# A graph network on one core: edges placed into 300 of 500 columns, counts in one product, and a factor of the attribute product in PSUM

## The chip, the core and the metric

The kernel runs on 1 core of a Trainium2 chip. The core has a matmul engine (TensorE; PE in the profile), three engines for elementwise work (VectorE or DVE, ScalarE or ACT, GpSimd or POOL) and a queue of its own for transfers (SyncE, SP). They run beside each other and wait for each other by semaphores. All work in SBUF, a memory of 128 partitions; matmuls write to PSUM, eight banks of 512 floats a partition. The metric is the device time of one call in microseconds (us).

## The reference

A graph has 3125 nodes with 128 features and 53125 directed edges, sorted by destination. Each edge has one of 8 types and 16 attributes. Four graph networks follow one another with layer norms between them; what matters here, shortened:

```python
h = relu(x @ proj.T + b)
for l in range(2):                                   # L0: gated graph network
    trans = einsum('nh,tdh->tnd', h, edge_W[l])
    agg = segment_sum(trans[edge_type, src], dst)    # one message per edge, by type and sender
    h = relu(gru_cell(agg, h, ...))
...                                                  # L1: three relational layers, means per type
    norm = 1 / max(counts[type, dst], 1)
    agg = segment_sum(xw[type, src] * norm, dst)
...                                                  # L2: normalised convolution over dst -> src
by_src = segment_sum(edge_attr, src) / count         # L3: two means of the attributes,
by_dst = segment_sum(edge_attr, dst) / count         #     by sender and by receiver
out = layernorm(x + mlp(concat(x, by_src, by_dst)))
```

All is float32.

## The kernel before

Edges are handled in 52 groups of 1024 (8 tiles of 128, one edge a partition). Nodes as senders lie in 25 sender blocks of 126.

**The first loop** (52 groups, 4 per pass of a hardware loop, about 105 to 865 us) does two things. It sums the messages of layer 1, and it builds the lists that the later layers use. For group g:
- GpSimd fetches 8 tiles of messages from the table in HBM by row number (L495 through `rows_of`, eight indirect DMAs, four buffers). The row numbers are put ready by ScalarE (`stage`, L964), two groups ahead.
- VectorE builds the 0/1 matrices of sender block (L1246) and of receiver (`onehot`, L1228), and the running number of each edge in its sender block (L1249, L1259 to L1271). From the number follows the edge's slot: a lane (`slot_lane`) and a column (`slot_col`) of a 128x500 map; a sender block has 20 columns of 128 lanes. It builds the 0/1 matrix of the lane times the edge's payload (`lane1h`, L1276).
- ScalarE builds the 0/1 matrix of the column, 8 tiles of 500 columns, as relu(1 - |column number - slot_col|): eight activations (L980) and one over 4000 columns (L984).
- TensorE multiplies, in this order: running numbers (L594, L595), message sums (`msg` x `onehot`, L600), counts by type and attribute sums by receiver (`mark` x `onehot`, L605, 24 rows), counts by sender block (`sb1h` x `onehot`, L608, 25 rows), and then `place` for the group before: `lane1h` x column matrix, 8 products of 500 columns that add into bank 7 of PSUM (L580). Each float32 product shows as two matmul records, so `place` shows as 16.
- VectorE adds the message sums and the two count results to `acc` and `nodes` (L1282, L1286, L1288).

Each step waits for its inputs by semaphores (`sb_known`, `rank_mm`, `slot_known`, `tile_ready`, `lane_ready`, `placed`, `summed`, `count_mm`), and buffers come in twos or fours.

**After it** `slots` reads the map, and four layers follow (about 900 to 2700 us). Each has a first part with 125 chunks of 4 columns (x1 records built on TensorE, copied by ScalarE, stored by SP), and a second part in which GpSimd fetches records and TensorE sums them by window (L731).

**The convolution stage** (about 2770 to 3490 us) has 100 steps `g`. GpSimd fetches 5 tiles of rows for a step (L495, `gmsg`, four buffers, 500 indirect DMAs in all), VectorE builds 5 matrices (`ghot`, L1667), TensorE multiplies them (L892). Spread over the first 88 steps lie the 52 attribute groups `attr(a)`: VectorE builds the sender block matrix `hi` (L1640) and sixteen products `aprod` = hi x attributes (L1646, two buffers), ScalarE the lane matrix `alane` (L1094, L1099), and TensorE multiplies (L899, 16 records of 400 columns a group). The order is written out in the code of each engine; no scheduler changes it. A flag set by `judge` sends the kernel to a general path, which is far slower, if an edge found no place.

## Time and profile before

| | |
|---|---|
| Time, median of 3 runs | 3567.47 us (3558.71 to 3567.86) |
| Time of the profiled execution | 3572.71 us |
| its span | 3570.9 us |
| TensorE matmul busy, share of the span | 2926.1 us, 82% |
| VectorE | 2001.8 us, 56% |
| ScalarE | 1064.1 us, 30% |
| GpSimd | 1558.0 us, 44% |

The profiled execution took 1.8 us more than its span, and 5.2 us more than the median. Busy shares are means over stages of quite different kind, so they do not say what bounds a stage. In a chain of waits the words "another core or an unknown queue", and in a list of waits "remote", stand where the profile knows no releaser.

### The profile page before, as it was taken

What the parts mean: (1) busy time and instruction counts of PE and PEld (TensorE: products, weight loads), DVE (VectorE), ACT (ScalarE), POOL (GpSimd) and SP (SyncE); (2) the same over time, 40 slices, a digit from 0 to 9 for tenths busy, and PEclk for the clock granted to TensorE, in tenths of its full rate; (3) what the DMA queues carried; (4) which work ended last, traced back from release to release, by engine and by line L of the source; (5) the groups of instructions that cost most, each with busy time, mean ns of one, the idle gap of its engine ahead of it and who ended that gap; (6) DMA issues with size and microseconds to landing.
All of it is one profiled execution on the core that took longest, in us unless ns stands there. A gap on an engine that the chain in (4) does not pass through costs nothing.

```text
span 3570.9 us, 49106 instructions
## 1 busy us (share of the span) xinstructions
PE 2926.1 (82%) x16338; PEld 2340.9 (66%) x16338; DVE 2001.8 (56%) x6739; ACT 1064.1 (30%) x1751; POOL 1558.0 (44%) x1641
## 2 busy tenths in 40 slices
PE   6799999899766998878997799878997767777748
PEld 2556665555665995777996799877996544444435
DVE  5445555555446775746764777435773754545514
ACT  2465566565332112340014300242001322323201
POOL 1455545551022661005640166103662677777760
PEclk8899999999887999999999999999996888887867
DMA  6111111110475661577767777677771122222211
GB/s 236 41 42 45 43 40 45 42 43 20 143 240 174 177 174 46 190 251 219 234 174 261 233 233 233 185 245 228 230 223 38 49 51 54 51 54 51 48 46 24
DMA packets 229115, 460.27 MB, mean 129 GB/s; under 512 B 40682, under 2 KB 95338, under 8 KB 228397
## 3 DMA queue, kind: packets, MB, share of 16 engines
q0 software_dynamic: 76992, 217.59, 22.5%
q1 hardware_dynamic: 151924, 240.14, 21.0%
q8 instruction: 112, 1.84, 0.2%
q14 instruction: 87, 0.70, 0.1%
HBM read 309.93 MB, written 147.65 MB: 128 GB/s over the span
## 4 chain that ended last, share of the span: by engine, by line
PE 53%; DMA 14%; POOL 13%; issue 8%; DVE 5%; another core or an unknown queue 4%; ACT 3%; SPq 0%; DVEq 0%; ACTq 0%; POOLq 0%
PE ps L731 20%; POOL gmsg L495 13%; DMA chunks<-xs 13%; PE ps L580 10%; PE ps L717 5%; PE ps L600 2%; ACT xs L1000 2%; PE ps L605 2%; PE ps L608 2%; PE ps L706 2%; PE ps L750 1%; PE ps L765 1%; PE ps L756 1%; PE ps L666 1%
## 5 line engine op out<-in xcount | busy, mean ns | idle before, releaser
L495 POOL DMA_INDIRECT rec<-chunks,idx x596 | 580.7, 974 | 965.4 <-DMA chunks<-xs 652.4
L731 PE MATMUL ps<-dhot,rec 128*128 128x168 f32 x4768 | 718.3, 311 | 65.3 <-DMA rec<-chunks,idx 24.7
L731 PEld LDWEIGHTS ps<-dhot,rec 128*128 128x128 f32 x4768 | 695.7, 193 | 86.5 <-issue 54.2
L1494 DVE TENSOR_SCALAR dhot<-iota,dcode 128x168 f32<-128x168 f32 x2384 | 568.9, 306 | 191.7 <-PE ps L731 110.8
L706 PE MATMUL ps<-hrow,shot 126*128 126x128 f32 x4000 | 518.6, 291 | 176.7 <-ACT xs L1000 139.3
L495 POOL DMA_INDIRECT gmsg<-gcn_rows,gcn_idx x500 | 545.5, 1091 | 269.2 <-issue 148.1
L706 PEld LDWEIGHTS ps<-hrow,shot 126*128 126x128 f32 x4000 | 492.9, 204 | 202.1 <-ACT xs L1000 161.6
L495 POOL DMA_INDIRECT msg<-messages,idx_buf x416 | 398.2, 957 | 430.2 <-ACT idx_buf L964 303.8
L580 PE MATMUL ps<-big,lane1h 128*128 128x500 f32 x848 | 392.0, 604 | 40.2 <-issue 38.3
L1000 ACT ACTIVATE xs<-ps 128x512 f32<-128x512 f32 x500 | 289.6, 597 | 423.8 <-DMA chunks<-xs 307.3
L1479 DVE TENSOR_SCALAR shot<-srow,lane_no 126x512 f32<-126x512 uint8 x500 | 237.7, 485 | 312.6 <-PE ps L706 246.2
L899 PE MATMUL ps<-aprod,alane 128*128 128x400 f32 x832 | 337.0, 557 | 40.9 <-issue 36.1
L980 ACT ACTIVATE tmp<-iota,slot_col 128x500 f32<-128x500 f32 x416 | 256.3, 698 | 336.1 <-DVE slot_col L1271 171.6
L580 PEld LDWEIGHTS ps<-big,lane1h 128*128 128x128 f32 x848 | 159.4, 194 | 243.0 <-issue 243.0
L892 PE MATMUL ps<-ghot,gmsg 128*128 128x126 f32 x1000 | 165.9, 321 | 161.1 <-DMA gmsg<-gcn_rows,gcn_idx 116.6
L899 PEld LDWEIGHTS ps<-aprod,alane 128*128 128x128 f32 x832 | 175.3, 217 | 180.1 <-issue 89.4
L892 PEld LDWEIGHTS ps<-ghot,gmsg 128*128 128x128 f32 x1000 | 152.8, 230 | 186.3 <-issue 167.9
L1646 DVE TENSOR_TENSOR aprod<-ahi,amark 128x208 f32<-128x208 f32 x832 | 235.5, 357 | 1.8
L1009 ACT ACTIVATE acc<-ps,bias 128x252 f32<-128x252 f32 (+1 forms) x39 | 18.0, 461 | 701.0 <-PE ps L720 647.3
L1667 DVE TENSOR_SCALAR ghot<-iota,gcn_lo 128x126 f32<-128x126 f32 x500 | 109.3, 299 | 180.0 <-remote 119.3
L1099 ACT ACTIVATE alane<-tmp,w 128x1024 f32<-128x1024 f32 x52 | 59.7, 1149 | 484.1 <-remote 215.9
L984 ACT ACTIVATE big<-tmp,w 128x4000 f32<-128x4000 f32 x52 | 188.8, 3630 | 1.7
(239 smaller groups left out, 2861.2 us busy)
## 6 DMA issues: line engine op xcount, KB each, us to landing
chunks<-xs SPq DMA_DIRECT2D x375, 256.0 KB, 4.6
tmp<-inverse_counts SPq DMA_DIRECT2D x36, 1008.0 KB
chunks<-xs SPq DMA_DIRECT2D x125, 258.0 KB, 4.5
srow<-lanes_of_slots SPq DMA_DIRECT2D x100, 320.0 KB, 4.3
messages<-big SPq DMA_DIRECT2D x25, 504.0 KB
rec<-chunks,idx POOLq DMA_INDIRECT x596
gmsg<-gcn_rows,gcn_idx POOLq DMA_INDIRECT x500
msg<-messages,idx_buf POOLq DMA_INDIRECT x416
```

Source lines behind the costliest of these rows:

```text
L495: eng.indirect_dma_start(buf, None, table, bass.IndirectOffsetOnAxis(ap=index, axis=0)).then_inc(sem, 16)
L580: last = mm(ps[:, 7, 0:NTILE], lane1h[:, slot, t, :], big[:, slot, t * NTILE:(t + 1) * NTILE], start=False, stop=False, skip_group_check=True)
L706: last = mm(ps[:, STAGE1_BANKS[i % 3], j * P:(j + 1) * P], shot[0:BS, i % SS, j * P:(j + 1) * P], hrow[0:BS, sb_, :], start=True, stop=True)
L731: last = mm(ps[:, 4 + i % 2, (v % 3) * WT:(v % 3 + 1) * WT], rec[:, v % RS, j * P:(j + 1) * P], dhot[:, v % DS, j * WT:(j + 1) * WT], star ...
L892: last = mm(in_chunk(ps[:, b // CB, :], b // CB, b), gmsg[:, g % MSLOTS, t, :], ghot[:, g % 3, t, :], start=c % (4 * QS) == 0, stop=c % (4 ...
L899: last = mm(ps[:, 7, 0:TB * A], alane[:, a % 2, t, :], aprod[:, a % 2, t, :], start=a == 0 and t == 0, stop=a == NG - 1 and t == G - 1)
L980: last = act(away[:, t * NTILE:(t + 1) * NTILE], iota[:, 0:NTILE], ACT.Abs, scale=-1.0, bias=slot_col[:, s, t:t + 1])
L984: act(big[:, s % 2, 0:G * NTILE], away, ACT.Relu, scale=-1.0, bias=wt("ones")[:, 0:1])\
L1000: act(xs[:, i % XS, 0:4 * P], ps[:, STAGE1_BANKS[i % 3], :], ACT.Copy).then_inc(q("x1_evac"), 1)
L1479: vec.tensor_scalar(shot[0:BS, i % SS, :], srow[0:BS, s_ % NS, (i % QS) * SPAN:(i % QS + 1) * SPAN], lane_no1[0:BS], None, ALU.is_equal).t ...
L1494: last = vec.tensor_scalar(dhot[:, v % DS, j * WT:(j + 1) * WT], iota[:, 0:WT], dcode[:, v, j:j + 1], None, ALU.is_equal)
L1646: last = vec.tensor_tensor(aprod[:, a % 2, t, b0 * A:b1 * A].rearrange("p (b a) -> p b a", a=A), hi[:, t, b0:b1].unsqueeze(2).to_broadcast ...
```

## The change

- `NEAR` = 300 columns. The map's columns are numbered anew: column = 100 x (running number // 512) + 4 x sender block + (running number & 3), where it was 20 x block + 4 x (number // 512) + (number & 3). Edges of one time then have columns near each other, and a group is placed into 300 columns that begin at 0, 100 or 200. TensorE's loop is written three times, for passes 0 to 5, 6 to 9 and 10 to 12 (`SEGMENTS`), ScalarE's five times.
- Types, attributes and sender blocks lie in one buffer `marks` of 56 columns, so that the two count products become one, and so do VectorE's two additions. ScalarE copies the attributes into it; VectorE writes the sender blocks a second time, in another order. A new semaphore `attr_kept` tells TensorE and SP of the copy.
- The zeros that start bank 7 come from the buffer of `lane1h`, and VectorE waits for the stored table before it clears half of `big`.
- `slots` counts the placed edges and `judge` compares their number with 53125.
- In the convolution stage `hi` is written to bank 6 of PSUM instead of SBUF (one buffer for two). Steps fetch the same tiles as before, under their new column numbers (`gcn_tile`).
- The 125 chunks of a layer are worked in the new order, and each is stored at the place in HBM where it lay before.

```diff
+QCOLS = 4 * TB
+NEAR = 3 * QCOLS
+SEGMENTS = ((0, 6), (6, 10), (10, PASSES))
...
-            big = one("big", [P, 2, 4096])
+            big = one("big", [P, 2, G * NEAR])
+            marks = one("marks", [P, 2, G, MC])
...
+        def near_passes():
+            for at, (p0, p1) in enumerate(SEGMENTS):
+                ends_here = at < len(SEGMENTS) - 1
+                yield p0, p1 - ends_here, [at] * SUB
+                if ends_here:
+                    yield p1 - 1, p1, [at] * (SUB - 1) + [at + 1]
...
-                        last = mm(ps[:, 7, 0:NTILE], lane1h[:, slot, t, :], big[:, slot, t * NTILE:(t + 1) * NTILE],
+                        last = mm(ps[:, 7, at * QCOLS:at * QCOLS + NEAR], lane1h[:, slot, t, :],
+                                  big[:, slot, t * NEAR:(t + 1) * NEAR],
                                   start=False, stop=False, skip_group_check=True)
...
+                            eng.wait_ge(q("attr_kept"), g + 1 + SUB)
                             for t in range(G):
-                            mm(ps[DST_ROWS, 2 + s % 2, 0:P], mark[:, s, t * TC:(t + 1) * TC], onehot[:, s % 2, t, :],
-                               start=t == 0, stop=t == G - 1)
-                        for t in range(G):
-                            last = mm(ps[SB_ROWS, 2 + s % 2, 0:P], own[:, :, t + 1], onehot[:, s % 2, t, :],
+                                last = mm(ps[COUNT_ROWS, 2 + s % 2, 0:P], marks[:, s % 2, t, :], onehot[:, s % 2, t, :],
...
+                            eng.wait_ge(q("count_mm"), g + (SUB - 1))
+                            act(marks[:, s % 2, :, MT + T:], by_group(mark[:, s, :], TC)[:, :, T:], ACT.Copy)\
+                                .then_inc(q("attr_kept"), 1)
                             eng.wait_ge(q("slot_known"), g + 1)
                             eng.wait_ge(q("tile_ready"), g + 1)
                             for t in range(G):
-                            last = act(away[:, t * NTILE:(t + 1) * NTILE], iota[:, 0:NTILE], ACT.Abs, scale=-1.0,
+                                last = act(away[:, t * NEAR:(t + 1) * NEAR], iota[:, ats[s] * QCOLS:ats[s] * QCOLS + NEAR], ACT.Abs, scale=-1.0,
                                            bias=slot_col[:, s, t:t + 1])
...
+                        vec.tensor_tensor(marks[:, s % 2, :, 0:TB], over_lanes(iota[:, 0:TB], G), over_tiles(src_sb[:, tiles], TB),
+                                          ALU.is_equal)
...
-                        st.did(vec.tensor_tensor(nodes[DST_ROWS, ds(base, P)], nodes[DST_ROWS, ds(base, P)],
-                                                 ps[DST_ROWS, 2 + s % 2, 0:P], ALU.add))
-                        vec.tensor_tensor(nodes[SB_ROWS, ds(base, P)], nodes[SB_ROWS, ds(base, P)],
-                                          ps[SB_ROWS, 2 + s % 2, 0:P], ALU.add).then_inc(q("counted"), 1)
+                        vec.tensor_tensor(nodes[COUNT_ROWS, ds(base, P)], nodes[COUNT_ROWS, ds(base, P)],
+                                          ps[COUNT_ROWS, 2 + s % 2, 0:P], ALU.add).then_inc(q("counted"), 1)
...
             def attr(a):
                 if a >= 2:
                     eng.wait_ge(q("attr_mm"), a - 1)
-                hi = by_group(ahi[:, a % 2, :], TB)
+                if a >= 1:
+                    eng.wait_ge(q("attr_prod"), a)
+                hi = by_group(ps[:, 6, P:P + G * TB], TB)
```

TensorE, one group inside the first loop, before:

```order
L594 MATMUL ps<-sb1h,w 128x200
L595 MATMUL ps<-sb_seen,w 128x200
L600 MATMUL ps<-onehot,msg 128x128 x8
L605 MATMUL ps<-onehot,mark 24x128 x8
L608 MATMUL ps<-onehot,sb1h 25x128 x8
L580 MATMUL ps<-big,lane1h 128x500 x8
```

The same group of the changed kernel, where the loop bodies have their own line numbers:

```order
L615 MATMUL ps<-sb1h,w 128x200
L616 MATMUL ps<-sb_seen,w 128x200
L621 MATMUL ps<-onehot,msg 128x128 x8
L625 REGISTER_ALU
L627 MATMUL ps<-onehot,marks 56x128 x8
L599 MATMUL ps<-big,lane1h 128x300 x8
```

Eight products went, eight became 300 columns wide, and nothing changed its place.

ScalarE, one group inside the first loop, before:

```order
L964 ISA
L964 ACTIVATE idx_buf<-row_idx 128x8
L980 ACTIVATE tmp<-iota,slot_col 128x500 x8
L984 ACTIVATE big<-tmp,w 128x4000
L963 REGISTER_ALU
```

and in the changed kernel:

```order
L982 ISA
L982 ACTIVATE idx_buf<-row_idx 128x8
L1000 ACTIVATE marks<-mark 128x8x16
L1005 ACTIVATE tmp<-iota,slot_col 128x300 x8
L1009 ACTIVATE big<-tmp,w 128x2400
```

The copy of the attributes stands behind the row numbers and ahead of the column matrix of the same group.

VectorE, where the convolution stage begins (one step with an attribute group), before:

```order
L1667 TENSOR_SCALAR ghot<-iota,gcn_lo 128x126 x5
L1640 TENSOR_TENSOR ahi<-iota,src_sb 128x200
L1646 TENSOR_TENSOR aprod<-ahi,amark 128x208
L1646 TENSOR_TENSOR aprod<-ahi,amark 128x192
L1646 TENSOR_TENSOR aprod<-ahi,amark 128x208
```

and now:

```order
L1703 TENSOR_SCALAR ghot<-iota,gcn_lo 128x126 x5
L1676 TENSOR_TENSOR ps<-iota,src_sb 128x200
L1682 TENSOR_TENSOR aprod<-ps,amark 128x208
L1682 TENSOR_TENSOR aprod<-ps,amark 128x192
L1682 TENSOR_TENSOR aprod<-ps,amark 128x208
```

The instructions and their order are the same; the sixteen products read their first factor from PSUM.

## Rows read from the trace of the kernel before

**Rows 1.** The page: the span, then busy time of each engine.
```profile
span 3570.9 us, 49106 instructions
PE 2926.1 (82%) x16338; PEld 2340.9 (66%) x16338; DVE 2001.8 (56%) x6739; ACT 1064.1 (30%) x1751; POOL 1558.0 (44%) x1641
```
**Rows 2.** Windows: first loop, convolution stage; total, PE, PEld, DVE, ACT, POOL, clock, DMA.
```profile
105.00:865.00 760.00, 690.33 (x3501) 449.38 (x3502) 384.80 (x1638) 450.08 (x519) 375.38 (x392) 0.97 0.15 40
2773.00:3488.00 715.00, 489.94 (x1844) 323.74 (x1842) 356.61 (x1375) 171.96 (x442) 525.74 (x479) 0.81 0.22 51
```
**Rows 3.** Timeline of TensorE, one group: start, length, line.
```profile
518.02 0.50 PE L595 MATMUL ps<-sb_seen,w 128*128 128x200 f32 x2
520.24 1.60 PE L605 MATMUL ps<-onehot,mark 128*24 128x128 f32 x13
...
523.45 6.97 PE L580 MATMUL ps<-big,lane1h 128*128 128x500 f32 x16
...
530.60 0.50 PE L595 MATMUL ps<-sb_seen,w 128*128 128x200 f32 x2
```
**Rows 4.** The same view, the group before it, and the loop's last places.
```profile
508.46 9.39 PE L580 MATMUL ps<-big,lane1h 128*128 128x500 f32 x16
...
851.39 13.68 PE L580 MATMUL ps<-big,lane1h 128*128 128x500 f32 x32
```
**Rows 5.** Timeline of VectorE, the group of rows 3; idle time before it in brackets.
```profile
518.56 0.36 DVE L1259 TENSOR_TENSOR rank_prod<-sb1h,ps 128x200 f32<-128x200 f32 x1 [5.71 <-PE ps L595]
...
520.36 0.17 DVE L1271 SCALAR_TENSOR_TENSOR slot_col<-src_sb,rank_f 128x8 f32<-128x8 f32 x1
...
523.67 0.28 DVE L1286 TENSOR_TENSOR nodes<-nodes,ps 24x128 f32 x1 [0.85 <-PE ps L608]
...
524.87 0.37 DVE L1246 TENSOR_TENSOR sb1h<-iota,src_sb 128x200 f32<-128x200 f32 x1
...
527.36 0.21 DVE L1253 TENSOR_TENSOR mark<-typ_f,iota 128x64 f32<-128x64 f32 x1
```
**Rows 6.** Groups by line, 400 to 800 us: count, busy, mean ns, idle before.
```profile
L495 POOL DMA_INDIRECT msg<-messages,idx_buf x222 | 212.6, 957 | 187.9 <-ACT idx_buf L964 123.1 <-issue 64.8
L980 ACT ACTIVATE tmp<-iota,slot_col 128x500 f32<-128x500 f32 x224 | 138.0, 698 | 164.2 <-issue 100.3 <-DVE slot_col L1271 63.9
L984 ACT ACTIVATE big<-tmp,w 128x4000 f32<-128x4000 f32 x28 | 101.7, 3631 | 0.9
...
L964 ACT ACTIVATE idx_buf<-row_idx 128x8 int32 x27 | 5.2, 193 | 0.0
```
**Rows 7.** Timeline of GpSimd, first fetch of the fourth group.
```profile
113.18 0.94 POOL L495 DMA_INDIRECT msg<-messages,idx_buf  x1 [13.96 <-ACT idx_buf L964]
```
**Rows 8.** Groups by line, convolution stage, 2773 to 3488 us.
```profile
L495 POOL DMA_INDIRECT gmsg<-gcn_rows,gcn_idx x479 | 525.7, 1098 | 205.1 <-issue 142.0 <-remote 37.1 <-PE ps L892 26.0
L899 PE MATMUL ps<-aprod,alane 128*128 128x400 f32 x832 | 337.0, 557 | 40.9 <-issue 36.1 <-DVE aprod L1646 4.8
...
L892 PE MATMUL ps<-ghot,gmsg 128*128 128x126 f32 x972 | 161.2, 321 | 158.8 <-DMA gmsg<-gcn_rows,gcn_idx 116.6 <-issue 41.0 <-DVE ghot L1667 1.0
L1646 DVE TENSOR_TENSOR aprod<-ahi,amark 128x208 f32<-128x208 f32 x414 | 151.8, 367 | 1.8
```
**Rows 9.** One line's instructions: shortest, median, longest ns; first and last start.
```profile
L495 POOL DMA_INDIRECT gmsg<-gcn_rows,gcn_idx x500: 938/944/3847, 2732.3 to 3488.1; - x167
```
**Rows 10.** Timelines of VectorE and GpSimd, convolution stage.
```profile
2913.39 4.58 DVE L1646 TENSOR_TENSOR aprod<-ahi,amark 128x208 f32<-128x208 f32 x16
...
2916.05 2.74 POOL L495 DMA_INDIRECT gmsg<-gcn_rows,gcn_idx  x1 [0.30 <-issue]
```
**Rows 11.** Timelines of GpSimd and VectorE in the second part of a layer.
```profile
1704.79 1.01 POOL L495 DMA_INDIRECT rec<-chunks,idx  x1 [0.30 <-issue]
...
1704.91 0.67 DVE L1512 TENSOR_TENSOR agg_rows<-ps,tmp 128x504 f32<-128x504 f32 x1
1705.50 1.01 DVE L1494 TENSOR_SCALAR dhot<-iota,dcode 128x168 f32<-128x168 f32 x4
```

More of the change, by code:

```diff
@@ L582, in place @@
                     last.then_inc(q("placed"), 1)
+                eng.wait_ge(q("zeros"), 1)
                 eng.sem_inc(q("count_mm"), SUB)
                 eng.sem_inc(q("placed"), 1)
[L586 to L613 removed]
@@ L691, in spread_slots @@
                 for i in range(NQ):
-                    sb_ = i // QS
-                    if i % QS == 0 and sb_ % CB == 0:
+                    sb_ = i % TB
+                    if i < TB and sb_ % CB == 0:
                         after(eng, "rows_kept", k, sb_ // CB + 1)
@@ L700, in spread_slots @@
                         eng.wait_ge(q("flags_known"), 1)
-                        mm(ps[:, 6, 256:261], wt("ones"), flags[:], start=True, stop=True).then_inc(q("flags_mm"), 1)
+                        mm(ps[:, 6, 256:262], wt("ones"), flags[:], start=True, stop=True).then_inc(q("flags_mm"), 1)
                     if i >= 3:
@@ L860, in _ @@
             for b in range(TB):
-                last = mm(ps[0:BS, 3, b:b + 1], block_of(nodes, b)[32:32 + T], wt("ones")[32:32 + T, 0:1], start=True,
+                last = mm(ps[0:BS, 3, b:b + 1], block_of(nodes, b)[TYPE_ROWS], wt("ones")[TYPE_ROWS, 0:1], start=True,
                           stop=True)
@@ L966, in first_loop @@
             def first_loop():
[L967 removed]
+                away = tmp_flat[:, 0:G * NEAR]
                 for s in range(AHEAD):
                     stage(s, s)
+                eng.wait_ge(q("zeros"), 1)
+                eng.sem_inc(q("attr_kept"), SUB)
                 all_stored(eng, 0)
                 eng.sem_inc(q("tile_ready"), 1)
[L972 to L986 removed]
```

156 lines of the change are left out of this document (86 added, 70 removed).

## The prediction

> **What bounds the kernel now.** I read the page first. TensorE is busy for 82% of the span, but that is a mean [rows 1]. Windows then split the span. Two stages hold what the change touches: the first loop, 760 us from 105 to 865, and the convolution stage, 715 us from 2773 to 3488 [rows 2]. The four layers between them keep their instructions and sizes; their chunks only come in another order and land at their old addresses, so I count them at nothing.
>
> In the first loop TensorE is busy for 690 of 760 us, and the others for 375 to 450 [rows 2]. The timeline shows one group in which nothing was late: from one running number product to the next 530.60 - 518.02 = 12.58 us [rows 3]. Times 52 groups that is 654 us, so 106 us (2.0 us a group) are halts and slow stretches, such as the 16 placing products that took 9.39 us where the next ones took 6.97 [rows 3, 4]. I have no cause for the halts. VectorE meanwhile waited 5.71 us for TensorE in the group [rows 5], and GpSimd waited 123 us of 400 for row numbers from ScalarE [rows 6]. TensorE's own length of a group is the bound.
>
> In the convolution stage TensorE is busy for 490 of 715 us and at a mean clock of 0.81 [rows 2]. GpSimd is the full one: 479 fetches with 525.7 us busy and 142.0 us of issue gaps make 668 of 715 us [rows 8]. Its median fetch takes 0.944 us, its mean 1.098, its longest 3.847 [rows 8, 9]. The timeline shows when one is long: VectorE ran its sixteen attribute products from 2913.39 to 2917.97, and a fetch begun at 2916.05 took 2.74 us, to 2918.79 [rows 10].
>
> **First loop, part by part.** Placing: 500 columns take 0.42 us a record (32 in 13.68 us, less the last one's tail) [rows 4]; 128 columns take 0.10 (the 32 count records from 520.24 to 523.45) [rows 3]. Between them lie 0.86 ns a column, so 300 columns take 0.25, and sixteen records save 16 x 0.17 = 2.75 us a group. These two rows enclose the new width. Counts: 16 of 32 records go, at 0.10 each 1.6 us. With 56 weight columns a record could cost 0.12, as the 128 wide ones do (16 between 518.02 + 0.34 and 520.24) [rows 3]; that would give back 0.3. I take 0.10. TensorE's group is then 12.58 - 2.75 - 1.6 = 8.2 us.
>
> The others, to see which is late next. ScalarE: an activation of 500 columns holds it 138.0 / 224 = 0.616 us, and 4000 columns take 3.63; the slope between 0.698 and 3.631 is 0.84 ns a column [rows 6]. Eight of 300 columns make 3.6 us, one of 2400 makes 2.3, the row numbers 0.19 [rows 6]. The copy of 128 attribute columns is not in the trace: at least 0.19 (8 columns), at most 0.70 (500 columns) [rows 6]; I take 0.3. The sum is 6.4 us. VectorE: from 518.56 to the end of its last instruction at 527.57 are 9.0 us, 0.85 of it a wait; one addition goes (0.28) and one 200 column comparison comes (0.37) [rows 5]: 8.3 us. GpSimd: (212.6 + 64.8) / 222 = 1.25 us a fetch, eight make 10.0 us a group [rows 6]. So fetching is late next, at 10.0, and TensorE stands at 8.2 plus halts.
>
> Two bounds meet. Fetching: the fourth group's fetches began at 113.18, held up by ScalarE [rows 7], which will be some 2.7 us earlier; 49 groups from 110.5 at 10.0 end at 600, and the last sums, counts and two placings (1.9 + 1.6 + 8.0 and a landing) end at 614. TensorE: 52 x (8.2 + 2.0) = 530 from 105 ends at 635, if halts keep their size a group. Row numbers are put ready two groups ahead and four buffers are there, so a halt of TensorE mostly doesn't stop fetching, and the two don't add. Three first passes through loop code instead of one, and more pieces on ScalarE, I price at 5 us, no row shows it. I take 640 for the end, and a gain of 225. At best it is 865 - 614 = 251; if halts and fetches add, 52 x 12.0 = 624 from 105, 136.
>
> The added wait: TensorE's counts wait for ScalarE's copy (`attr_kept`). Behind it are the placing and the next running numbers, for which VectorE waits. ScalarE gets there when the group before is done: 1.8 us (518.56 to 520.36 [rows 5]) for VectorE's column numbers, 5.9 for its own work, 0.5 for row numbers and copy, in all 8.2 us after the former running numbers, while the counts stand at 10.0 + 1.9. That hides it by 3.7 us.
>
> Start and `slots`: VectorE's memsets change by under 1 us beside fetches. `slots` gets eight small instructions and `judge` four, of 0.17 to 0.5 us each; VectorE is waited for there. I put 3 us on the path; nothing if they are hidden, 5 if none is.
>
> **Convolution stage.** No instruction goes. The first factor of the sixteen products moves to PSUM, and the question is whether a fetch beside them then runs free. The nearest row is exactly of that form: L1512 of a layer reads PSUM first and SBUF second, 504 columns, and the fetch begun just ahead of it took 1.01 us [rows 11]. So the fetches fall towards 0.944: 479 x (1.098 - 0.944) = 74 us. TensorE is waited for more often then: its 498 us of products [rows 8] must fit into some 650 rather than 715, with a clock that was 0.81. I give 12 us of the 74 back. Bounds: nothing, if PSUM changes nothing, and 95, if the 37.1 us of GpSimd's unnamed waits [rows 8] shrink too. I take 62. The wait for the one `hi` buffer is for VectorE's own earlier work, done long before.
>
> A rule against it: the Trainium skill ("VectorE: DVE Perf Modes", section on the TRN2 errata) gives VectorE 58 cycles plus the columns for an SBUF input and 120 plus the columns for a PSUM input. By it 832 products would cost VectorE 54 us more. The trace disagrees: the PSUM instruction of 504 columns let the next one start after 1705.50 - 1704.91 = 0.59 us [rows 11], which is 58 + 504 cycles and not 624.
>
> **Sum.** The profiled execution took 3572.7 us. 3572.7 - 225 - 62 + 3 = 3289. The median of the runs is 5 us below the profiled time, so I predict 3285.
>
> **Rivals.**
>
> Fetches stay blocked. For: VectorE's first factor was never shown to be the cause; it could be the second input, or the writes to SBUF. Against: fetches beside L1512 were short [rows 11], one row of one instruction, not a run of sixteen. Then only the first loop gains: 3347. The Trainium skill ("SBUF — State Buffer", "Who interferes with whom") has both sides: two SBUF inputs hold up a GpSimd instruction that reads SBUF, yet it infers that the making of DMA descriptors only needs the write side, so that `tensor_tensor` would not hold it up. By the second half nothing is gained here; the 2.74 us fetch beside such a run [rows 10] speaks for the first.
>
> Halts and fetches add, or TensorE, with waits now, gets the lower clock more often. For: the clock was 0.97 in the loop and 0.81 where TensorE waits more [rows 2]. Against: fetching runs ahead by two groups. The loop then takes some 11.3 us a group and gains 170; total 3340.
>
> Both go better. Halts shrink with the number of instructions and the convolution stage gains 90: the loop is bound by fetches alone, 3235.
>
> Slower than before. The groups get one more handoff, ScalarE's copy, and three engines in a ring; if a late semaphore there stops them as in the halts, each such stop holds all three. The gain of 290 is gone when a group stops 290 / 52 = 5.6 us longer, on top of today's 2.0; at 6.5 us the time is 3615. Nothing in the profile shows stops of that size in every group.
>
> The change doesn't do what it says. An edge outside its 300 columns is lost, `judge` sees it, and the general path takes thousands of us. I worked out the running numbers from the reference's edges: at the steps (groups 24 and 40) they lie between 681 and 1078 and between 1202 and 1732, and the windows hold up to 1535 before the first step, 512 to 2047 between, 1024 and more after the second. No edge is lost.
>
> **How the numbers follow.** Forecast 3285: 0.54, on its own 3245 to 3325. Halts or clock, 3340: 0.17. Fetches stay blocked, 3347: 0.12. Both better, 3235: 0.13. Slower: 0.03, the general path in it with under 0.01. The last 0.01 is for no change. The range 3215 to 3365 takes in the first four, with a loop gain between 136 and 251 and a stage gain between 0 and 95, less the corners where both are at an end. A measurement of this kernel tells about 0.3% (11 us) from no change. Faster 0.96, the same 0.01, slower 0.03.
>
> **What would show it.** First loop from 105 to about 640, distance of two groups about 10.2 us, GpSimd's waits for row numbers nearly gone, placing records 0.25 us apart, the count row with 56 rows 16 times a group. Convolution stage: longest fetch near 1.1 us in place of 3.85, mean 0.95, stage some 650 us, clock no lower. Layers within a few us. It is wrong if a group takes over 11 us, if long fetches stay beside the sixteen products, or if the parts between 900 and 2700 us change in length by more than 15 us.

## The result, and the profile after

The changed kernel took 3598.53 us (median of 8 runs, 3578.85 to 3611.82), the kernel before 3562.44 us in 8 runs beside it. The ratio is 1.0107, 95% interval 1.0065 to 1.0149: 1.1% slower. Forecast were 3285 us, a range up to 3365 and a chance of 0.03 for slower.

The same kernel before took 3562 us in the runs of the result and 3608 us in one later job (a job is a set of runs taken together on one chip), but 3342 to 3379 us in eight other jobs; I call these the condition with halts and the one without. The changed kernel was run whole once with halts, which is the result above, and in two jobs without, where it was over 5% faster than the kernel before. Each experiment is compared with the kernel before in its own job.

First the profile of the result. The page of the changed kernel, its first three rows as in [rows 1]:

```profile
span 3610.0 us, 47619 instructions
...
PE 2816.9 (78%) x15506; PEld 2339.6 (65%) x15506; DVE 1994.9 (55%) x6749; ACT 936.6 (26%) x1803; POOL 1486.3 (41%) x1641
```

TensorE has 109 us less work than in [rows 1], and the span is 39 us longer: the time is in waits. The windows of the two stages, which answer to [rows 2]:

```profile
105.00:903.00 798.00, 556.37 (x2683) 442.55 (x2682) 381.06 (x1636) 321.56 (x567) 375.60 (x392) 0.80 0.15 38
2835.00:3526.00 691.00, 506.62 (x1849) 316.89 (x1848) 352.24 (x1378) 172.53 (x442) 459.47 (x480) 0.80 0.25 53
```

The last placing ends at 902.5 us instead of 865.1, so the first loop lost 37 us; the prediction had it gain 225. Compared with the kernel before, from there to the first fetch of a layer it is 14 us more, the layers take 10 more, the convolution stage (first to last fetch) takes 731.4 instead of 755.7 us, a gain of 24 where 62 were forecast, and the tail 2 more: 37 + 14 + 10 - 24 + 2 = 39.

In the loop, one group is as short as worked out, and the next is not. TensorE's timeline over two groups ("issue" in the brackets is idle time for which the profile shows no wait):

```profile
517.73 0.50 PE L616 MATMUL ps<-sb_seen,w 128*128 128x200 f32 x2
518.07 1.95 PE L621 MATMUL ps<-onehot,msg 128*128 128x128 f32 x16
519.94 1.95 PE L627 MATMUL ps<-onehot,marks 128*56 128x128 f32 x16
521.83 4.31 PE L599 MATMUL ps<-big,lane1h 128*128 128x300 f32 x16
...
526.42 0.50 PE L616 MATMUL ps<-sb_seen,w 128*128 128x200 f32 x2
526.76 1.98 PE L621 MATMUL ps<-onehot,msg 128*128 128x128 f32 x16
530.59 0.27 PE L627 MATMUL ps<-onehot,marks 128*56 128x128 f32 x1 [1.86 <-issue]
531.33 0.30 PE L627 MATMUL ps<-onehot,marks 128*56 128x128 f32 x1 [0.47 <-issue]
533.42 0.37 PE L627 MATMUL ps<-onehot,marks 128*56 128x128 f32 x1 [1.80 <-issue]
...
541.82 2.23 PE L627 MATMUL ps<-onehot,marks 128*56 128x128 f32 x8 [1.03 <-issue]
543.98 5.09 PE L599 MATMUL ps<-big,lane1h 128*128 128x300 f32 x16
548.91 0.50 PE L615 MATMUL ps<-sb1h,w 128*128 128x200 f32 x2
```

From one L616 to the next are 526.42 - 517.73 = 8.69 us (forecast 8.2; [rows 3] had 12.58). Then the merged counts come one by one, 0.7 to 2.1 us apart, and the next group's L615 starts at 548.91, 22.9 us after that of the halted group at 525.98. GpSimd and VectorE over the same stretch:

```profile
519.90 0.95 POOL L514 DMA_INDIRECT msg<-messages,idx_buf  x1 [11.62 <-ACT idx_buf L982]
...
538.88 0.95 POOL L514 DMA_INDIRECT msg<-messages,idx_buf  x1 [0.30 <-issue]
551.39 0.95 POOL L514 DMA_INDIRECT msg<-messages,idx_buf  x1 [11.56 <-ACT idx_buf L982]
```

```profile
518.80 0.36 DVE L1283 TENSOR_TENSOR rank_prod<-sb1h,ps 128x200 f32<-128x200 f32 x1
...
542.60 0.36 DVE L1283 TENSOR_TENSOR rank_prod<-sb1h,ps 128x200 f32<-128x200 f32 x1 [14.71 <-remote]
544.38 0.17 DVE L1295 SCALAR_TENSOR_TENSOR slot_col<-src_sb,rank_f 128x8 f32<-128x8 f32 x1
```

GpSimd fetched two groups back to back, 519.90 to 539.83; VectorE got the running numbers of L616 at 542.60, though their record ended at 526.92. "remote" here is not another core: the trace's semaphore updates show `placed`, `rank_mm` and `summed` of these records arriving within 0.25 us of each other, at 542.5 to 542.7. TensorE's matmuls went on at full pace at 541.82 and its signals came at 542.5, both only after the last fetched rows had landed (541.1). Only then do VectorE and ScalarE go on, and ScalarE's next row numbers let GpSimd begin the next pair at 551.39. So two groups take 551.39 - 519.90 = 31.5 us. The waits of the whole loop, each with its total, times and longest:

```profile
ACT tmp L1005 <- DVE slot_col L1295: 444.8, 39, 17.6
POOL msg L514 <- ACT idx_buf L982: 290.5, 27, 11.9
DVE rank_prod L1283 <- remote: 249.7, 24, 16.1
...
PE ps L627 <- issue: 138.1, 130, 2.5
```

GpSimd's wait for ScalarE, which was to vanish, is there every second group.

In the convolution stage the PSUM factor did what it was to do. By line, 2835 to 3526 us, as in [rows 8], then the one line's shortest, median and longest, as in [rows 9]:

```profile
L514 POOL DMA_INDIRECT gmsg<-gcn_rows,gcn_idx x480 | 459.9, 958 | 247.7 <-issue 136.6 <-remote 80.5 <-PE ps L910 30.6
L917 PE MATMUL ps<-aprod,alane 128*128 128x400 f32 x832 | 367.5, 578 | 104.3 <-issue 92.3 <-DVE aprod L1682 11.5
```

```profile
L514 POOL DMA_INDIRECT gmsg<-gcn_rows,gcn_idx x500: 941/947/1342, 2794.1 to 3525.5; - x167
```

The longest fetch fell from 3.85 to 1.34 us and the mean from 1.098 to 0.958, which freed 66 us of GpSimd. But its waits for a free buffer (remote and L910; only TensorE's L910 frees one) rose from 63 to 111 us, and TensorE's unexplained idle time ahead of the attribute products from 36 to 92: what the shorter fetches freed went into waits for TensorE.

### The profile page after: what moved, and what is told of

Same layout as the page of the kernel before. It is cut to its first block, busy times and chain, and to the rows that moved or that the text cites. A ratio compares the mean times of both kernels' runs of the same rounds, so it can differ in the third digit from the quotient of the medians.

```text
span 3610.0 us, 47619 instructions
## 1 busy us (share of the span) xinstructions
PE 2816.9 (78%) x15506; PEld 2339.6 (65%) x15506; DVE 1994.9 (55%) x6749; ACT 936.6 (26%) x1803; POOL 1486.3 (41%) x1641
## 4 chain that ended last, share of the span: by engine, by line
PE 56%; DMA 14%; issue 12%; DVE 6%; another core or an unknown queue 5%; POOL 4%; ACT 3%; SPq 0%; DVEq 0%; ACTq 0%; POOLq 0%
PE ps L750 19%; DMA chunks<-xs 13%; PE ps L599 6%; PE ps L917 5%; PE ps L736 5%; POOL gmsg L514 4%; PE ps L627 4%; PE ps L621 3%; PE ps L725 2%; ACT xs L1025 2%; PE ps L910 2%; DVE aprod L1682 2%; PE ps L769 1%; PE ps L784 1%
## 5 line engine op out<-in xcount | busy, mean ns | idle before, releaser
L514 POOL DMA_INDIRECT gmsg<-gcn_rows,gcn_idx x500 | 478.8, 958 | 311.7 <-issue 142.4
L917 PE MATMUL ps<-aprod,alane 128*128 128x400 f32 x832 | 367.5, 578 | 104.3 <-issue 92.3
L1005 ACT ACTIVATE tmp<-iota,slot_col 128x300 f32<-128x300 f32 x416 | 187.4, 534 | 485.9 <-DVE slot_col L1295 459.5
L627 PE MATMUL ps<-onehot,marks 128*56 128x128 f32 x832 | 155.3, 329 | 144.4 <-issue 138.1
L599 PE MATMUL ps<-big,lane1h 128*128 128x300 f32 x848 | 250.9, 453 | 0.1
L627 PEld LDWEIGHTS ps<-onehot,marks 128*56 128x56 f32 x832 | 116.4, 157 | 184.8 <-issue 180.6
L1682 DVE TENSOR_TENSOR aprod<-ps,amark 128x208 f32<-128x208 f32 x832 | 231.9, 360 | 1.8
L599 PEld LDWEIGHTS ps<-big,lane1h 128*128 128x128 f32 x848 | 171.2, 208 | 67.4 <-issue 24.9
L910 PEld LDWEIGHTS ps<-ghot,gmsg 128*128 128x128 f32 x1000 | 144.3, 219 | 83.2 <-issue 71.8
L910 PE MATMUL ps<-ghot,gmsg 128*128 128x126 f32 x1000 | 150.7, 305 | 57.2 <-issue 37.2
```

What stands on the lines that cost most here:

```text
L514: eng.indirect_dma_start(buf, None, table, bass.IndirectOffsetOnAxis(ap=index, axis=0)).then_inc(sem, 16)
L599: last = mm(ps[:, 7, at * QCOLS:at * QCOLS + NEAR], lane1h[:, slot, t, :], big[:, slot, t * NEAR:(t + 1) * NEAR], start=False, stop=False, ...
L627: last = mm(ps[COUNT_ROWS, 2 + s % 2, 0:P], marks[:, s % 2, t, :], onehot[:, s % 2, t, :], start=t == 0, stop=t == G - 1)
L910: last = mm(in_chunk(ps[:, b // CB, :], b // CB, b), gmsg[:, g % MSLOTS, t, :], ghot[:, g % 3, t, :], start=(g * GT + t) % (4 * QS) == 0, ...
L917: last = mm(ps[:, 7, 0:TB * A], alane[:, a % 2, t, :], aprod[:, a % 2, t, :], start=a == 0 and t == 0, stop=a == NG - 1 and t == G - 1)
L1005: last = act(away[:, t * NEAR:(t + 1) * NEAR], iota[:, ats[s] * QCOLS:ats[s] * QCOLS + NEAR], ACT.Abs, scale=-1.0, bias=slot_col[:, s, t:t ...
```

## What a halt is, counted from the traces

A run of fetches (first to last landing with no gap over 2 us) is a window. I counted the matmul records that TensorE has in each window. Kernel before, 180 to 860 us: 45 windows of 7.7 to 10.0 us, one group each, hold 27 to 58 records, mean 50. Changed kernel, the same stretch: 19 windows of about 19 us, two groups each, hold 42 to 50 records, mean 46. Two groups of the changed kernel are 104 records: some 46 in the window of 19 us, the other 58 in the 12.5 us without a fetch, and that is the 31.5 us.

What is a limit in this, and what isn't, shows beside a run without halts. The kernel before with one part changed (the first loop untouched) has windows of 9.0 to 9.2 us there that hold 49 records, and four of about 19 us that hold 89 to 91. So 19 us could hold twice what they held in the changed kernel, but 50 records in 9 us are what TensorE does anyway, and the counts of the kernel before show no limit at 50. Its halts show in the time of a group, 14.8 instead of 12.6 us. They are short and stand at the windows' ends: three in a row end at 321.6, 335.3 and 348.8 us, where the windows end at 321.6, 335.2 and 348.3. With VectorE's waits for late signals (up to 12.7 us) they are the 106 us for which the prediction had no cause.

One more thing tells the conditions apart. Each fetch gives 16 landing updates, 6656 in the loop. Without halts the trace has 6643 of them in the changed kernel, with halts 1378, and 1828 in the kernel before. The page shows it too, as a time to landing that is there or missing (the layers' fetches, first with halts, then in a run of the same kernel without):

```profile
rec<-chunks,idx POOLq DMA_INDIRECT x596
...
rec<-chunks,idx POOLq DMA_INDIRECT x596, 3.9
```

All four traces with halts lack it, all others have it. So the windows above are measured from the landings that are on record; from the packets of the same queue they come out about half a us longer.

Theory A: under indirect fetches in flight TensorE gets through some 50 records and then halts till the window ends, and its signals come late; a faster TensorE lets GpSimd's fetches of two groups run together, which doubles the window and not what fits in it. Rival B: a ring inside the loop (row numbers behind ScalarE's columns, the supply of instructions) sets the pace whatever is fetched.

## The experiments

**No fetches at all.** In both kernels, the first loop's fetches are left out and messages are zeros:

```diff
-                    for t in range(G):
-                        rows_of(msg[:, s, t, :], table_rows, idx_buf[:, s, t:t + 1], q(f"gathered_{s}"))
-                            eng.wait_ge(q(f"gathered_{s}"), (it + 1) * (16 * G))
+                            eng.wait_ge(q("rows_known"), g + 1)
```

> The changed kernel with the 416 indirect fetches of its first loop left out (messages are zeros; everything else in the loop stays). Theory A: TensorE gets on by only some 50 matmul passes once an indirect fetch is in flight and then halts until the last of its landings; without fetches no halt is left, a group takes what a clean one takes (548.91 to 557.49: 8.6 us), the first loop ends at about 105 + 52 x 8.7 = 560 us instead of 902, and the kernel takes about 3260 us. Rival B: the pace of 15.4 us per group comes from a ring inside the loop (row numbers that ScalarE hands out behind its columns, or TensorE's own supply of instructions), and stays without the fetches: 3580 to 3600 us.

> The kernel before with the same 416 fetches left out. Theory A: its clean group is 12.58 us; halts cost it about 2 us per group, so the loop ends at about 105 + 52 x 12.7 = 765 us instead of 865 and the kernel takes about 3460 us; the difference to the changed kernel without fetches is then the 205 us that the prediction expected. Rival B: 3540 to 3562 us, and the halts stay.

Measured, beside a kernel before of 3359.67 us: the changed kernel without fetches 3104.99 us (ratio 0.9253, 0.9234 to 0.9273), end of the last placing at 547 us; the kernel before without them 3364.64 us (1.0015, 0.9996 to 1.0035), last placing to 757. The unchanged kernel before was itself 200 us faster than in the result. Without fetches it gained nothing, against theory A's number, because here it had no halts to lose. So the run doesn't tell A from B; it gives the lengths of clean groups: from the first running number product to the last (737.7 - 95.8) / 51 = 12.6 us, and for the changed kernel (533.8 - 95.8) / 51 = 8.6 us. With the tail of the last group, (547 - 95) / 52, it is 8.7; the times per group below are worked out in this second way.

**One part alone.** The kernel before with only the PSUM factor, and the changed kernel with its placing at 500 columns:

```diff
-                hi = by_group(ahi[:, a % 2, :], TB)
+                if a >= 1:
+                    eng.wait_ge(q("attr_prod"), a)
+                hi = by_group(ps[:, 6, P:P + G * TB], TB)
```

```diff
-NEAR = 3 * QCOLS
-SEGMENTS = ((0, 6), (6, 10), (10, PASSES))
+NEAR = 5 * QCOLS
+SEGMENTS = ((0, PASSES),)
```

> The kernel before with one part of the change alone: the one-hot of the source blocks lies in PSUM while VectorE multiplies it by the attributes. The prediction put this part at -62 us, between 0 and -95. The changed kernel's convolution stage is only 24 us shorter (731.4 against 755.7 us). Theory A (fetches got cheaper, but TensorE halts under more of them): -20 to -35 us, about 3535 us. Rival B (the part is worth the 62 us, the rest of the change takes it back in this stage): about 3500 us.

> The changed kernel with its placing widened to all 500 columns again (one segment, merged counts and PSUM kept). Theory A: each window of fetches still lets TensorE issue about 50 passes, but a group of 11 us instead of 8.6 makes back-to-back fetches of two groups rarer, as in the kernel before: the loop ends between 830 and 880 us, kernel 3500 to 3550 us, faster than the changed kernel. Rival B (columns matter as the prediction had it, something else in the change stalls the loop): slower than the changed kernel by 50 us or more, above 3640 us.

Same job, so without halts. PSUM alone: 3296.56 us, ratio 0.9825 (0.9807 to 0.9843), 63 us, which is the size of rival B of that expectation. Its times were for a kernel before of 3562 us, so whether the part is worth as much with halts stays open. The first loop, with all its fetches, ends at 753.5 us, and no wait of TensorE is listed in it: the kernel before, too, has no halts here. The convolution stage's fetches by line, first without the part (the kernel before without its loop's fetches, whose stage is untouched), then with it, 2628 to 3214 us:

```profile
L495 POOL DMA_INDIRECT gmsg<-gcn_rows,gcn_idx x425 | 458.0, 1078 | 129.5 <-issue 129.2 <-PE ps L890 0.3
```

```profile
L494 POOL DMA_INDIRECT gmsg<-gcn_rows,gcn_idx x468 | 444.5, 950 | 142.6 <-issue 141.7 <-PE ps L891 0.9
```

Fetches are never kept waiting by TensorE here (0.3 and 0.9 us), so the shorter mean becomes 43 fetches more in the same 586 us. 500 columns with the rest of the change: 3232.35 us, ratio 0.9628 (0.9604 to 0.9653), last placing at 686, (686 - 93) / 52 = 11.4 us per group. Both theories' numbers for it were for the condition with halts, and it says nothing on those.

**The changed kernel again, its fetches held apart, and its counts unmerged.** One wait more on GpSimd in the second; in the third the product of `marks` in two sets of eight (and their two additions):

```diff
                     eng.wait_ge(q("idx_staged"), it * SUB + s + 1)
+                    eng.wait_ge(q("count_mm"), it * SUB + s + 3)
```

```diff
-                                last = mm(ps[COUNT_ROWS, 2 + s % 2, 0:P], marks[:, s % 2, t, :], onehot[:, s % 2, t, :],
-                                          start=t == 0, stop=t == G - 1)
+                                mm(ps[DST_ROWS, 2 + s % 2, 0:P], marks[:, s % 2, t, MT:], onehot[:, s % 2, t, :],
+                                   start=t == 0, stop=t == G - 1)
+                            for t in range(G):
+                                last = mm(ps[SB_ROWS, 2 + s % 2, 0:P], marks[:, s % 2, t, 0:TB], onehot[:, s % 2, t, :],
+                                          start=t == 0, stop=t == G - 1)
```

> The changed kernel once more, not edited. In the last runs the kernel before took 3360 us instead of 3562, and no matmul record of its first loop had a halt of the kind seen in the profiles shown. Theory A (the halts under fetches are a condition of the chip or of the moment, not of the kernel): where the kernel before takes about 3360 us, the changed one has no halts either, a group is bound by GpSimd's fetches (10.0 us), the first loop ends at about 105 + 52 x 10.1 = 630 us and the kernel takes 3140 to 3170 us, 6 % faster; where the kernel before takes about 3560 us, the changed one takes about 3600 us again. Rival B (the change itself makes the halts): 3500 us or more on any chip.

> The changed kernel with one wait more on GpSimd: the fetches of a group start only when the counts of the group two before are summed, so that those of two groups can't follow back to back. Theory A, where halts occur: each window of landings is 9 to 11 us long instead of 20, TensorE's 52 passes of a group nearly fit in what it may issue in one, a group takes 12 to 13 us instead of 15.4, the loop ends at 730 to 780 us and the kernel takes 3430 to 3490 us. Where no halts occur: within 10 us of the changed kernel, since GpSimd's 10.0 us per group bound both. Rival B (length of the window does not matter, only the sum of the fetch time): no better than the changed kernel where halts occur.

> The changed kernel with its counts summed by two sets of eight matmuls again (68 passes per group instead of 52; 300 columns and PSUM kept). The prediction gave the merging 1.6 us of TensorE per group. Theory A, where no halts occur: a group is 10.2 us on TensorE against 10.0 for the fetches, so +5 to +30 us against the changed kernel. Where halts occur, and a window lets TensorE issue some 50 passes: 16 passes more to be issued outside the windows or at the slow rate of 1.4 us each, +40 to +150 us. Rival B (halts depend on time, not on the number of passes): within 20 us of the changed kernel in both cases.

Measured beside a kernel before of 3350.19 us: the changed kernel 3169.72 us, ratio 0.9457 (0.943 to 0.9485); held apart 3188.05 us, 0.9519 (0.9494 to 0.9543); unmerged 3162.12 us, 0.9452 (0.9424 to 0.948). The change itself is worth 180 us without halts. Its loop there, windows from 105 to 618 us (the last placing's end), and the timelines of TensorE and GpSimd:

```profile
105.00:618.00 513.00, 450.97 (x2632) 371.12 (x2631) 375.68 (x1603) 314.59 (x556) 378.27 (x390) 0.99 0.22 59
```

```profile
406.86 0.50 PE L616 MATMUL ps<-sb_seen,w 128*128 128x200 f32 x2
408.54 2.05 PE L621 MATMUL ps<-onehot,msg 128*128 128x128 f32 x16 [1.18 <-DMA msg<-messages,idx_buf]
410.52 1.95 PE L627 MATMUL ps<-onehot,marks 128*56 128x128 f32 x16
412.40 4.31 PE L599 MATMUL ps<-big,lane1h 128*128 128x300 f32 x16
...
416.89 0.50 PE L616 MATMUL ps<-sb_seen,w 128*128 128x200 f32 x2
```

```profile
413.54 0.94 POOL L514 DMA_INDIRECT msg<-messages,idx_buf  x1 [0.30 <-issue]
414.79 0.94 POOL L514 DMA_INDIRECT msg<-messages,idx_buf  x1 [0.30 <-issue]
```

TensorE now waits for rows (1.18 us), GpSimd for nothing but its own 0.30 us: 416.89 - 406.86 = 10.03 us per group, the forecast's 10.0 of fetching. No matmul record waits for "issue", and every signal follows its record at once, though fetches are in flight nearly all the time: from 180 to 599 us no two landings lie over 2 us apart, one window with 2133 records. The 16 records saved by merging are worth nothing here because fetching is the bound (9.99 us per group with and without); the expectation had +5 to +30 us for it.

The wait that was to hold the fetches apart did not do so here, and its 18 us (the expectation allowed 10) have another cause. GpSimd's waits from 105 us to the end of its loop, all of them:

```profile
POOL msg L514 <- issue: 122.8, 403, 0.3
POOL msg L514 <- PE ps L628: 0.3, 1, 0.3
```

The new wait held it once, for 0.3 us, and from 180 to 599 us the landings follow each other with gaps under 2 us as before. But the first fetch starts at 88.95 us instead of 68.98, because the new wait also holds the first group until TensorE has reached its loop, and the loop ends 17 us later.

**Half the fetches, and plain transfers instead of indirect ones.** The first leaves four of eight tiles at zero; the second fetches neighbouring rows, so other messages:

```diff
-                    for t in range(G):
+                    for t in range(G // 2):
```

```diff
-                        rows_of(msg[:, s, t, :], table_rows, idx_buf[:, s, t:t + 1], q(f"gathered_{s}"))
+                        eng.dma_start(msg[:, s, t, :], table_rows[(s * G + t) * P:(s * G + t + 1) * P, :])\
+                           .then_inc(q(f"gathered_{s}"), 16)
```

> The changed kernel with only four of the eight indirect fetches of each group of the first loop (the other half of the messages are zeros). Where no halts occur (kernel before near 3355 us): the fetches take 5 us per group and TensorE's 8.6 us bound it, the loop ends at about 545 us instead of 614 and the kernel takes 3095 to 3110 us, as without any fetch. Where halts occur (kernel before near 3560 us): theory A (TensorE may issue some 50 passes under a window of fetches and halts after them until it ends) has windows of 5 us with at most 30 passes in them, so no halts in the loop: 8.6 us per group, the whole kernel some 330 us under the changed one. Rival B (any fetch in flight slows TensorE in proportion): half of the halts stay, 12 us per group.

> The changed kernel with the first loop's fetches as plain transfers of 128 neighbouring rows, issued by GpSimd like the indirect ones (so the messages are those of other rows). If the 1.25 us of a fetch lie in the handling of row numbers, a plain one is cheaper: where no halts occur TensorE's 8.6 us bound a group and the kernel takes about 3100 us; if they lie in making descriptors of any kind, about 3170 us as the changed one. Where halts occur: theory A1 (they belong to rows written in the background, whoever names them) keeps them, theory A2 (they belong to GpSimd's indirect fetches) does not.

This job met the condition with halts: kernel before 3607.81 us. Half the fetches: 3292.27 us, ratio 0.9123 (0.9006 to 0.924); plain transfers: 3259.34 us, 0.9032 (0.8914 to 0.9149). TensorE's waits in the half-fetch loop (two lines, the whole answer), and two groups of the loop with plain transfers:

```profile
PE ps L615 <- DVE sb_seen L1273: 31.4, 24, 1.9
PE ps L599 <- ACT big L1009: 0.2, 1, 0.2
```

```profile
401.00 0.50 PE L617 MATMUL ps<-sb_seen,w 128*128 128x200 f32 x2
...
409.59 0.50 PE L617 MATMUL ps<-sb_seen,w 128*128 128x200 f32 x2
...
418.17 0.50 PE L617 MATMUL ps<-sb_seen,w 128*128 128x200 f32 x2
```

No "issue" wait is left in either; with plain transfers no wait of TensorE at all is listed in the loop. In the half-fetch loop, with windows of 4 to 5 us, which hold up to 32 records, a group takes (583 - 93) / 52 = 9.4 us, 0.8 over a clean one and over theory A's 8.6: TensorE's signals still come late now and then, up to 2.8 us at VectorE's last addition. With plain transfers a group takes (542.5 - 91) / 52 = 8.7 us and the signals follow their records at once. Rival B above, the ring, is out: with the same ring, copies and instructions, the halts go when the indirect fetches get few or are replaced. Of the second expectation theory A2 fits, that the halts belong to indirect fetches, but only in part is it shown: plain transfers are issued faster (0.53 us instead of 0.95), so their windows also last just 4.2 us, and windows that short had no issue halts with indirect fetches either. What differs at equal length is the lateness of TensorE's signals (0.8 us a group against none) and the landings on record (1521 of 3328 against 6656 of 6656). Plain transfers in windows of 9 or 19 us were not run, nor the whole changed kernel in this job. The convolution stage, whose indirect fetches stayed, still took 738 us in both, against 629 without halts.

**For the condition with halts.** The three kernels of the last job without halts once more, and one kernel whose loop has four forms one after the other:

```diff
-            with eng.Fori(0, PASSES) as it:
+            for p0, p1, apart in ((0, 4, False), (4, 7, True), (7, PASSES, False)):
+                with eng.Fori(p0, p1) as it:
...
+                        if apart:
+                            eng.wait_ge(q("count_mm"), it * SUB + s + 3)
```

> The changed kernel a third time, beside the two that follow: so far it stands at 1.0107 of the kernel before where that takes 3562 us and at 0.9457 where it takes 3350 us. Theory A (one condition of the machine decides, seen in the kernel before's own time): one of these two pairs comes back within 1 %; with the slow kernel before there are halts of TensorE under the fetches and the loop ends near 900 us, with the fast one there are none and it ends near 614 us. Rival B (a spread of the changed kernel alone): the kernel before and the changed one move independently.

> The changed kernel with the fetches of two groups held apart, as in after_apart, which cost 18 us where no halts occur. Where halts occur: theory A (TensorE issues some 50 passes under a window of fetches, then halts until it ends) has one group's 52 passes per window of 9 to 10 us: 12 to 13 us per group, loop end at 730 to 780 us instead of 900, kernel 3430 to 3490 us, 0.96 to 0.98 of the kernel before. Rival B (the summed fetch time decides, not the length of a window): like the changed kernel, 3580 to 3610 us. Where no halts occur: 3180 to 3190 us.

> The changed kernel with its counts in two sets of matmuls (68 passes per group), which cost nothing where no halts occur. Where halts occur: theory A has 16 passes more than the 50 a window allows, so +40 to +150 us against the changed kernel of this call. Rival B (not the number of passes but time counts): within 20 us of it. Where no halts occur: 3155 to 3175 us.

> The changed kernel with four forms of its first loop one after the other: groups 0 to 15 as they are, 16 to 27 with the fetches of two groups held apart, 28 to 39 as they are, 40 to 51 with the counts in two sets of matmuls (68 passes instead of 52). Where no halts occur (kernel before near 3355 us): 10.1, 10.4, 10.1 and 10.3 us per group. Where halts occur (kernel before near 3560 us or above): theory A (some 50 passes can be issued per window of fetches, then TensorE halts until its end) gives 15.4, then 12 to 13, then 15.4, then 16.5 to 18 us per group. Rival B (the sum of the fetch time decides, not the length of its windows) gives 15.4 us held apart too. Rival C (time counts, not the number of passes) gives 15.4 us with two sets of counts too.

Measured beside 3367.76 us: 3186.95 us (0.9478, 0.9433 to 0.9524), 3211.62 (0.9551, 0.9508 to 0.9594) and 3180.27 (0.9463, 0.9416 to 0.9511): nearly the same three ratios as on the other chip, and again no halts. (Held apart it took 22 us more than the expectation had at most, with two sets 5 us more.) The mixed kernel ran in five jobs on five chips:

> The same kernel as after_mixed, for the condition with halts. Where no halts occur: 3177 to 3189 us again. Where halts occur, per group in its four parts: theory A 15.4, 12 to 13, 15.4, 16.5 to 18 us; rival B 15.4 us held apart too; rival C 15.4 us with two sets of counts too.

> The same kernel as after_mixed, for the condition with halts. Where no halts occur: 3170 to 3190 us again. Where halts occur, per group in its four parts: theory A 15.4, 12 to 13, 15.4, 16.5 to 18 us; rival B 15.4 us held apart too; rival C 15.4 us with two sets of counts too.

> The same kernel as after_mixed, for the condition with halts. Where no halts occur: 3155 to 3190 us again. Where halts occur, per group in its four parts: theory A 15.4, 12 to 13, 15.4, 16.5 to 18 us; rival B 15.4 us held apart too; rival C 15.4 us with two sets of counts too.

> The same kernel as after_mixed, for the condition with halts. Where no halts occur: 3155 to 3190 us again. Where halts occur, per group in its four parts: theory A 15.4, 12 to 13, 15.4, 16.5 to 18 us; rival B 15.4 us held apart too; rival C 15.4 us with two sets of counts too.

> The same kernel as after_apart. Where halts occur: theory A 3430 to 3490 us, faster than both kernels there; rival B 3580 to 3610 us. Where no halts occur: 3183 to 3215 us again.

It gave 0.9418 (0.9339 to 0.9498), 0.9433, 0.9411, 0.9492 and 0.9454, always beside a kernel before of 3342 to 3379 us; after_apart_3 gave 0.9563 (0.9466 to 0.9659). Its four parts took 9.6, 10.2, 10.2 and 10.3 us per group in the first of these runs, where the expectation had 10.1, 10.4, 10.1 and 10.3. None met halts, so both questions stay open: whether windows held apart would spare TensorE there, and whether records or time fill a window. None of these versions is shown to beat the changed kernel where there are no halts, and none of them was run where there are.

## Why the prediction was wrong, point by point

- TensorE's group, 12.58 to 8.2 us: right but for 0.5 us. It is 8.69 us in the clean group beside halted ones and 8.6 without any fetch; sixteen placing records take 525.98 - 521.83 = 4.15 us rather than 16 x 0.25 = 4.0, and the sixteen merged counts 1.89 rather than 1.6, the 0.3 that the prediction named and left out.
- ScalarE, VectorE and the added wait: right; `attr_kept` shows up as no wait of TensorE in any profile.
- Fetching late next at 10.0 us: right wherever TensorE doesn't halt (10.03; loop end 618 us, forecast 614 to 640).
- "TensorE: 52 x (8.2 + 2.0) ends at 635, if halts keep their size a group", and "a halt of TensorE mostly doesn't stop fetching, and the two don't add". **This step failed.** The halts were 15.6 - 8.7 = 6.9 us per group, not 2.0. They go with the indirect fetches (with half of them 0.8 us, with plain transfers none). With the shorter TensorE group the fetches of two groups follow each other, in windows of 19 us instead of 9; and with each halt TensorE's signals come late, and with them VectorE, ScalarE's row numbers and so the fetches after next. That the longer windows make the halts longer is how the traces read; no run with halts varied the length of the windows alone. Four buffers didn't help: the next row numbers are handed out in ScalarE's order, behind columns that wait for TensorE. Where the halts are missing the loop's gain is 753.5 - 618.3 = 135 us, not 225, as the kernel before then has none of its 106 us either.
- The convolution stage: the mechanism right, and its size too, without halts: 63 us measured, 62 forecast. The size is in part luck: the 62 were worked out from a profile with halts, where the stage took 756 us (686 without). With halts, 24: what the fetches gave, TensorE's halts took (36 to 92 us ahead of the attribute products). The prediction had given back 12 of 74 for that. Of the two readings weighed under "Fetches stay blocked", the one by which products with both inputs in SBUF hold a fetch up came true (mean fetch 1.078 us, with one input in PSUM 0.950).
- The rule weighed for VectorE's PSUM input: the trace goes on disagreeing. The sixteen-fold product with both inputs in SBUF took 367 ns at the mean [rows 8], with one in PSUM 360 with halts and 354 without.
- The rival on the other side had the place and nearly the price right (a group that stops 5.6 us longer in a ring of three engines; measured 6.9 instead of 2.0), and got 0.03 because "nothing in the profile shows stops of that size in every group". The profile did show what they go with: short halts end where a run of fetches has landed, three times in a row in the stretch counted above. An unexplained 106 us was carried over as a constant.
- The parts between were counted at nothing, with 3 us for `slots`, and were to stay within 15 us. With halts it was 24: 14 more from the loop's end to the layers' first fetch, 10 more in the layers. So this sign of being wrong came true as well; what made the 24 us no run separates. Without halts the first is 5 us, and the layers of all versions take 1553 to 1579 us (1559 and 1563 in the two versions of the kernel before), so no lengthening is shown there.
- Of the other signs, a group took 15.6 us where over 11 was to be wrong, and GpSimd's waits for row numbers stayed; no long fetches stayed.

## What to carry to other kernels

Idle time whose cause is unknown is no constant: before pricing a change that speeds one engine up, line its halts up with what the other engines have in flight, for a shorter period puts more of that into each microsecond. A buffer depth only decouples two engines if the hand-out of the next request doesn't stand in program order behind work that waits for the slower one. And a kernel at the edge of such an effect can gain 5% or lose 1% by the condition that it meets, so a comparison says which only for that condition, and the kernel before has to run beside each version.

## What the hardware showed that was not expected

The kernel before ran in ten jobs and took 3342 to 3379 us in eight of them and 3562 and 3608 us in two; its clean group of 12.6 us is the same in both conditions, and the first loop's difference (865 against 753.5 us) is TensorE's halts and late signals while indirect fetches land. The layers and the convolution stage, which fetch so too, are longer as well (1600 against 1563 us, 756 against 686). It isn't a property of one chip: the chip that ran the no-fetch kernels beside 3360 us ran the half-fetch one beside 3608 us some 15 minutes later. What makes the condition no run shows. In it, a window of 19 us of indirect fetches let 42 to 50 matmul records of the changed kernel pass (89 to 91 of the kernel before in as long a window without halts), the last of them trickle 0.7, 1.4 or 2.1 us apart, and TensorE's semaphore signals arrive up to 16 us after the record's end; VectorE's and ScalarE's signals in the same stretch, those that the trace has, come on time. Plain transfers of as many bytes, issued by the same engine in windows of 4.2 us, do none of this. The granted clock doesn't make the halts: the kernel before had them at 0.97; in the changed kernel it was 0.80 with halts, where TensorE had less to do, and 0.99 without.

One rival is open. The same traces lack most of the landing updates, and every run on record was taken with its span and clock, so none tells whether the halts occur when nothing is recorded: recording may slow the engines, or what slows them may also lose records. The supply of instructions is less likely: in the first loop the changed kernel's two instruction queues moved 11 packets, at times that have nothing to do with the halts' rhythm of 31.5 us.
